# x^T of the last feed-forward by small loads and VectorE transposes in place of TensorE's

## The reference, cut to what matters

```
def _L1_ffn_ref(x, W0, bias0, W1, bias1):
    B, L, H = x.shape
    X = x.reshape(-1, H).astype(jnp.float16)
    D = jnp.dot(X.astype(jnp.float32), W0.T) + bias0       # 512 -> 2048
    D = jax.nn.gelu(D, approximate=False).astype(jnp.float16)
    E = jnp.dot(D.astype(jnp.float32), W1.T) + bias1       # 2048 -> 512
    return E.astype(jnp.float16).reshape(B, L, H)
...
x = _layernorm(x + _L1_ffn_ref(x, ...), axis=-1)
```

## Time and profile before

| | |
|---|---|
| median of 3 runs | 2569.36 us |
| the profiled execution | 2567.99 us |
| its span, first to last instruction | 2566.3 us |
| granted TensorE clock, mean | 0.970 |
| busy: TensorE, VectorE, ScalarE, GpSimd | 2397.7, 1217.7, 808.5, 902.2 us |

### The profile page before, as it was taken

The page is one execution under the profiler, slowest core; times in us unless marked ns, Lnnn a source line. Parts: engine busy times, 40 slices in busy tenths (PEclk is TensorE's granted clock), DMA queues, the critical chain, the costliest instruction groups (busy, mean ns, idle before and its releaser), DMA issues. The chain is left out here.

```text
span 2566.3 us, 39680 instructions
## 1 busy us (share of the span) xinstructions
PE 2397.7 (93%) x12835; PEld 1794.6 (70%) x12835; DVE 1217.7 (47%) x2518; ACT 808.5 (32%) x1371; POOL 902.2 (35%) x1104
## 2 busy tenths in 40 slices
PE   7999899999999958599999995999999979999997
PEld 6887655555555536488888884788888858888886
DVE  3334477777777678511111115676864461111221
ACT  3222255555555521144444442010111012222221
POOL 2000155555555635233333333524334122222221
PEclk9999899999999979799999997999999989999999
DMA  6895254554554235311010103131411151000000
GB/s 238 286 293 180 103 129 118 125 127 119 124 128 119 63 140 196 135 34 49 33 49 33 66 17 128 57 118 46 153 39 69 58 177 33 33 33 33 33 33 33
DMA packets 154745, 255.38 MB, mean 100 GB/s; under 512 B 9904, under 2 KB 47792, under 8 KB 154672
## 3 DMA queue, kind: packets, MB, share of 16 engines
q1 hardware_dynamic: 137712, 208.20, 26.5%
q0 software_dynamic: 6400, 25.26, 3.2%
q10 hardware_dynamic: 10560, 20.97, 2.5%
HBM read 161.59 MB, written 92.27 MB: 99 GB/s over the span
## 5 line engine op out<-in xcount | busy, mean ns | idle before, releaser
L177 DVE CUSTOM_DVE_ANT_0 junk<-psum,causal 128x896 bf16<-128x896 f32 (+7 forms) x512 | 373.7, 751 | 169.9 <-PE psum L828 145.7
L929 ACT ACTIVATE p_probs<-psum 128x512 f32<-128x512 f32 (+1 forms) x640 | 318.0, 555 | 274.9 <-PE psum L841 270.0
L1378 POOL TENSOR_TENSOR p_h_lo<-p_h,p_h_hi 128x512 fp32r<-128x512 f32 x128 | 164.5, 1285 | 325.9 <-ACT p_h_hi L1407 325.9
L841 PE MATMUL psum<-qst,kst 98*128 98x512 f32 (+3 forms) x768 | 223.8, 371 | 6.2 <-POOL p_ones L701 5.7
L2031 POOL CAST p_h<-p_h 128x512 fp32r<-128x512 f16 x128 | 91.4, 714 | 374.2 <-ACT p_h L2055 374.1
L747 POOL TENSOR_SCALAR_AFFINE_SELECT p_probs<-p_probs 128x128 f32<-128x128 f32 x512 | 139.8, 296 | 230.2 <-ACT p_probs L929 227.8
L841 PEld LDWEIGHTS psum<-qst,kst 98*128 98x128 f32 x768 | 132.3, 191 | 111.7 <-DVE rowmax L177 42.7
L828 PE MATMUL psum<-kst,qst 96*128 96x128 f32 (+3 forms) x720 | 208.2, 364 | 0.0
L1075 PE MATMUL psum<-p_xT,p_w_hi 128*128 128x512 f32 x512 | 204.0, 398 | 0.7 <-ACT p_xT L2042 0.7
L1075 PE MATMUL psum<-p_xT_hi,tern 128*128 128x512 f32 x512 | 203.1, 397 | 1.4 <-DVE p_xT_lo L1477 1.4
L1446 PE MATMUL psum<-tern,p_h_hi 128*128 128x512 f32 x512 | 199.5, 390 | 2.3 <-POOL p_h_lo L1378 2.3
(11 more groups left out here) (192 smaller groups left out, 4659.6 us busy)
## 6 DMA issues: line engine op xcount, KB each, us to landing
qst<-q_parts SPq DMA_DIRECT2D x96, 256.0 KB, 4.8
kst<-k_parts SPq DMA_DIRECT2D x96, 256.0 KB, 7.0
q_parts<-p_qk_out SPq DMA_DIRECT2D x32, 512.0 KB, 3.4
k_parts<-p_qk_out SPq DMA_DIRECT2D x32, 512.0 KB, 3.4
ffn_x<-x SPq DMA_DIRECT2D x12, 1024.0 KB, 5.6
p_x<-in_x_t POOLq DMA_DIRECT2D x8, 1024.0 KB, 8.1
v_rows<-p_v_out SPq DMA_DIRECT2D x32, 256.0 KB, 4.0
v<-v_rows SPq DMA_DIRECT2D x16, 512.0 KB, 4.2
```

What stands on the lines that cost most here:

```text
L177: return dve.tensor_tensor_reduce(view(junk[:, 0:n]), bank, view(self.causal[:, SEQ - n:SEQ]), 1.0, FLOOR, ALU.add, ALU.max, self.rowmax[: ...
L841: mm = pe.matmul(psum[:, bank, col:col + CH - q0], kst[s][0:KD + 2, g, j * P:(j + 1) * P], qst[s][0:KD + 2, c, g, q0:CH], start=True, stop ...
L929: act.activation(probs[:, n % 2, g, col:CH], psum[:, banks_of(s, "s", st)[0], col:CH], ACT.Exp, scale=SM_SCALE).then_inc(p_ready, 1)
L1378: pool.tensor_tensor(h_lo[:, m % 2, :], h[:, m % 2, :], f32(h_hi[:, m % 2, :]), ALU.subtract).then_inc(hl_done, 1)
```

## The change

For all chunks but the first, TensorE's transposes, their banks and the cast from `x3` are gone. In their place:

- `load_pieces` issues 16 DMAs per chunk, one per group of 32 features (q) and feature block (k). Each writes 32 partitions with 16 runs of 32 features (128 bytes), so that partition 32q + j holds, for each of the 16 token groups m, the features of token 32m + j. 
- `turn` on VectorE transposes 32x32 squares within these pieces, four instructions of 128x512 fp32, which gives x^T, and casts it to fp16 into `x16` (now feature-major). 
- ScalarE copies `x16` from SBUF to `xT` after the steps t = 10 to 13 instead of from PSUM after t = 9 to 12.

Chunk 1's pieces are issued by ScalarE at the phase's start, behind its copies for chunk 0 and ahead of the Gelu table's load, into `res`; they are turned into `x3[1]` when VectorE has split all weights. The later chunks' pieces are issued by SyncE, those of chunk n + 2 in chunk n, once chunk n + 1 has been cast, ahead of the reload and the store of chunk n. They go to the first two slots of `stage` and are turned into the other two, behind the LayerNorm of chunk n. SyncE's load of `x3[1]` now waits for chunk 1's cast. The first chunk is as before.

```diff
-        T = Banks(nc, ctx, "p6_tbank", psum, 6, 2, 2 * KT)
+        T = Banks(nc, ctx, "p6_tbank", psum, 6, 2, KT)
...
+        BL = 32
+        flat = lambda ap: ap.rearrange("p t d -> p (t d)")
+        second = (flat(res[:, :, :]), x3[1][:, :])
+        later = (flat(stage[:, 0:2, :]), flat(stage[:, 2:4, :]))
+
+        def load_pieces(eng, chunk, dst):
+            for q in range(P // BL):
+                for k in range(KT):
+                    to = dst[q * BL:(q + 1) * BL, k * CH:(k + 1) * CH].rearrange("j (m i) -> j m i", i=BL)
+                    cols = slice(k * P + q * BL, k * P + (q + 1) * BL)
+                    eng.dma_start(to, x3_dram[chunk].rearrange("(m j) d -> j m d", j=BL)[:, :, cols]).then_inc(x_split, 16)
...
@@ sync
+                sp.wait_ge(x_cast, 2)
                 load_x(0, 1)
                 def body(b, last):
                     for c in range(2):
+                        if not last:
+                            sp.wait_ge(x_cast, 2 * b + c + 2)
+                            load_pieces(sp, 2 * b + c + 2, later[0])
                         sp.wait_ge(ln.summed, ln.FROM + CT + 8 * b + 4 * c + 4)
@@ scalar
                 def x_T(b, c, k):
-                    m = KT * c + k
-                    T.wait_full(act, b, m)
-                    T.free(act.activation(xT[:, c, k, :], T.bank(m).bitcast(F16)[:, 0:CH], ACT.Copy), m)
+                    if k == 0:
+                        act.wait_ge(x_cast, 2 * b + c + 1)
+                    act.activation(xT[:, c, k, :], flat(x16[:, :, :])[:, k * CH:(k + 1) * CH], ACT.Copy).then_inc(x_ready, 1)
...
+                load_pieces(act, 1, second[0])
                 act.preload_act_table(ACT.Gelu)
...
-                            if HT // 2 < t <= HT // 2 + KT and not (c and last):
-                                x_T(b + c, 1 - c, t - HT // 2 - 1)
+                            if HT - 2 - KT <= t < HT - 2 and not (c and last):
+                                x_T(b + c, 1 - c, t - HT + 2 + KT)
@@ tensor
-                            if HT // 2 <= t < HT // 2 + KT and not (c and last):
-                                transposes(b + c, 1 - c, t - HT // 2)
@@ vector
+                def turn(chunk, pieces, turned):
+                    dve.wait_ge(x_split, 16 + 16 * KT * (P // BL) * chunk)
+                    for k in range(KT):
+                        part = slice(k * CH, (k + 1) * CH)
+                        dve.transpose(turned[:, part], pieces[:, part]).then_inc(x_turned, 1)
+                    dve.wait_ge(x_turned, KT * chunk)
+                    dve.wait_ge(x_ready, KT * chunk)
+                    dve.tensor_copy(flat(x16[:, :, :]), turned).then_inc(x_cast, 1)
...
+                turn(1, *second)
                 dve.wait_ge(bias_loaded, 16)
...
                         ln.vector_part(dve, 2 * b + c + 1, lambda t: res[:, t, :], lambda t: res[:, t, :])
+                        if not last:
+                            turn(2 * b + c + 2, *later)
```

More of the change, by code:

```diff
@@ L1977, in phase_ffn1 @@
         passed = sem("p6_passed")
-        x_cast = sem("p6_x_cast")
+        x_cast, x_ready = sem("p6_x_cast"), sem("p6_x_ready")
+        x_split, x_turned = sem("p6_x_split", 16), sem("p6_x_turned")
         h_done, h_used = sem("p6_h_done", 2), sem("p6_h_used", 1)
         stored = sem("p6_stored", 1)
+        BL = 32
[8 more added lines that the diff above has]
+                    eng.dma_start(to, x3_dram[chunk].rearrange("(m j) d -> j m d", j=BL)[:, :, cols]).then_inc(x_split, 16)
         with nc.Block() as block:
@@ L2039, in x_T @@
                 def x_T(b, c, k):
-                    m = KT * c + k
-                    T.wait_full(act, b, m)
-                    T.free(act.activation(xT[:, c, k, :], T.bank(m).bitcast(F16)[:, 0:CH], ACT.Copy), m)
+                    if k == 0:
+                        act.wait_ge(x_cast, 2 * b + c + 1)
+                    act.activation(xT[:, c, k, :], flat(x16[:, :, :])[:, k * CH:(k + 1) * CH], ACT.Copy).then_inc(x_ready, 1)
                 for k in range(KT):
-                    x_T(0, 0, k)
+                    T.wait_full(act, 0, k)
+                    act.activation(xT[:, 0, k, :], T.bank(k).bitcast(F16)[:, 0:CH], ACT.Copy).then_inc(x_ready, 1)
+                load_pieces(act, 1, second[0])
                 act.preload_act_table(ACT.Gelu)
@@ L2062, in _, with transposes @@
                 pe.wait_ge(built, 2)
[L2064 to L2067, removed]
+                def transposes(k):
+                    pe.wait_ge(x_cast, 1)
+                    if k >= 2:
+                        pe.wait_ge(x_ready, k - 1)
                     for t in range(CT):
-                        mm = pe.transpose(T.bank(m).bitcast(F16)[:, t * P:(t + 1) * P], x16[:, t, k * P:(k + 1) * P], ident16[:, :])
-                    T.fill(mm, m)
+                        mm = pe.transpose(T.bank(k).bitcast(F16)[:, t * P:(t + 1) * P], x16[:, t, k * P:(k + 1) * P], ident16[:, :])
+                    T.fill(mm, k)
                 def hidden(b, c, t):
                     if t == 0:
-                        for k in range(2):
-                            T.wait_freed(pe, k, 4 * b + 2 * c + 2)
+                        pe.wait_ge(x_ready, KT * (2 * b + c + 1))
                     pe.wait_ge(w_done, blocks.index(("w0", t // 2)) + 1)
@@ L2082, in _ @@
                 for k in range(KT):
-                    transposes(0, 0, k)
+                    transposes(k)
                 hidden(0, 0, 0)
@@ L2119, in _ @@
                 dve.memset(ln.meanvar[:, :, :], 1.0).then_inc(ln.got_mean, CT)
[L2121 to L2127, removed]
+                def turn(chunk, pieces, turned):
[6 more added lines that the diff above has]
+                    dve.tensor_copy(flat(x16[:, :, :]), turned).then_inc(x_cast, 1)
+                dve.wait_ge(x_loaded[0], 16)
+                dve.tensor_copy(flat(x16[:, :, :]), x3[0][:, :]).then_inc(x_cast, 1)
                 for i, (which, n) in enumerate(blocks):
@@ L2138, in body @@
                     for c in range(2):
-                        if not (c and last):
-                            cast(b + c, 1 - c)
                         for a in range(CT):
@@ L2144, in body @@
                             Y.free(dve.tensor_tensor(e16[:, a, :], Y.bank(m), b1r[:, :], ALU.add), m)
+                        dve.wait_ge(x_loaded[c], 16 * b + 16)
                         dve.wait_ge(stored, 1 + 32 * b + 16 * c)
```

## The result

The changed kernel takes 2577.0 us (median of 7 runs, 2574.69 to 2580.27) against 2569.36 (seven runs by now, same median): ratio 1.0032, 95% interval 1.002 to 1.0043. It is slower by 7.6 us, where 2.1 us less was forecast. The profiled execution took 2576.99 us.

The account below looks back on a forecast made before the run. The prediction took TensorE to bound the last feed-forward, apart from its start. Gain -9.1, idle time +4.4 and slow restart +2.6 made -2.1 us: 2567.3 us against the median of 2569.36, range 2561.5 to 2588.

Parts of the forecast that it names:

- The gain: Last feed-forward, TensorE: seven chunks lose four transpose groups each at 0.325 us, 9.1 us in all.
- The price of 16 issues: Phase start, ScalarE's queue: 0.5 us per load issue, 8.0 us in all, ahead of the Gelu table's load.
- The idle time: Phase start: TensorE gets its first h 4.4 us late and idles that long (3.0 and 7.6 at the ends).
- the 2.6 us for the clock: Phase start: TensorE's matmuls restart slowly after the idle time, adding 2.6 us; nothing is the other end.
- the main case: Whole change: 2.1 us less, own range -4 to +3 us, chance 0.42.
- R2: Phase start: the queue fills and ScalarE is held; +15 us with 8 loads held, +3 with 12; chance 0.23.
- The second term of R2: Draining one load: 32 packets per DMA engine, each taking turns with a weight packet, 3.1 us.
- Pieces for chunk 1: Chunk 0: at 30 ns a packet the pieces land at 2113 to 2118, narrowly before the 2120.5 deadline.
- the doubling of the 30 ns: 128-byte packets: read-modify-write might double the price, to about 30 us a chunk; no row showed it.
- R3: Chunk 0, t = 10: chunk 1's pieces come late at 60 ns a packet, +10 us; chance 0.13.
- R4: Steady chunks: above some 130 ns a packet each of six chunks stalls, +20 us or more; chance 0.05.
- Costed at nothing: Beside other work: chunk 1's pieces, steady-chunk loads and the output store, VectorE's turn, ScalarE's copies from SBUF; no cost.

Follow-up runs that it names:

- f1_spread: Against the changed kernel, chunk 1's 16 loads are issued two behind each of chunk 0's Gelus t = 0 to 7; 2559.4 us, 0.9963 of the kernel before.
- d2_wide: Changed kernel with chunk 1's 16 loads of 64 KB in whole 2 KB rows instead of pieces, for timing only; 2566.15 us (one run).
- f2_sync: Changed kernel with chunk 1's 16 loads on SyncE's queue behind the weights, none on ScalarE's; 2559.55 us, 0.9963 of the kernel before.
- d4_alone: Changed kernel, but SyncE issues the weight blocks from the fifth on only when chunk 1's pieces have landed; 2568.74 us (one run).
- d3_four: Changed kernel with chunk 1's same pieces in four loads of 2048 packets instead of 16 of 512, at the same place; 2575.37 us (one run).
- d5_first8: Changed kernel with 8 of chunk 1's 16 loads at ScalarE's place and 8 on SyncE's queue behind the weights; 2565.97 us (one run).

## Why the prediction was wrong, point by point

**The gain: right.** 9.1 us forecast, 9.0 measured in the chunk's length and 9.3 in f1_spread. The chunk went to 58.0 us.

**The price of 16 issues: the step that failed.** "I take 0.5, with 0.41 and 0.7 as ends. Then 16 x 0.5 = 8.0 us." It was 19.48 us. The idle time was 15.2 us where the sum had 4.4, and the 2.6 us for the clock were 2.2. With d2_wide's 0.46 us an issue the sum comes out as forecast, -2.2 against -2.1. The price of an issue was read from rows in which nothing was held, and it is a price for a queue with room. The 2577.0 us lie inside the stated range, but only because the slow rivals had stretched it to 2588; the main case had the wrong sign.

**R2 was the mechanism, with the wrong unit.** It asked how many loads can be outstanding. The nine of the earlier trace rows were the evidence (their issues are 0.37 to 0.67 us, not the "0.4 to 0.5 us only" of the prediction, which decides nothing), but in their whole stretch, 1565 to 1572, the queue moved 1151 packets, 72 per DMA engine; here it was to hold 512. The room lies near 100 to 160 packets per DMA engine: three loads of 32 went in freely, and the first to be held was the fourth (1.04 us here, 1.86 in f2_sync) or the fifth (2.39 in d4_alone). As an estimate, at one load per 1.22 us and 6.3 us to landing about five are under way. The landings of the changed kernel's start:

```profile
p_stage<-in_f_w SPq DMA_DIRECT2D x9, 512.0 KB, 7.3
p_out<-x ACTq DMA_DIRECT2D x16, 64.0 KB, 6.3
```

The second term of R2 was off as well, and the other way: 3.1 us to drain a load was 1.3. The DMA queues in a stretch of the hold (packets, MB, share of 16 engines), weights and pieces:

```profile
q1 hardware_dynamic: 1315, 1.78, 82.7%
q10 hardware_dynamic: 2979, 0.37, 32.9%
```

A piece's packet takes 0.329 x 120 us / 2979 = 13 ns, not 30, and 2979 of them pass beside 1315 of the weights, not one for one. R2's +15 us for eight held loads is therefore two errors that partly cancel. What happened is a room for four or five loads, and 1.2 us on average for each of the sixteen, +8.6 us by the balance. The chance of 0.23 was too small for a queue whose depth no row showed.

The Trainium skill's account (Perfetto Trace Analysis, DMA Instruction — HWDGE (DVE, Sync)), that the issue lasts until the descriptors are generated and that the buffer may be full before, agrees with the trace: issues grew to 2.78 us, and to 6.3 us with four times the packets (d3_four). It was cited, and given too little weight; the same load issued in 0.35 us into a queue with room, so the generating alone isn't what takes long. Its other part, a generator locked for one issuer at a time, does not show in SyncE's issues of the same time:

```profile
L2010 SPq DMA_DIRECT2D p_stage<-in_f_w x10: 367/368/368, 2073.0 to 2094.7; - x10
...
DMA to landing us min/median/max: 5.6/7.1/8.1
```

They stay at 0.37 us while ScalarE is held; those at 2076.37 and 2087.25 fall into issues of ScalarE of 2.05 and 2.78 us. So one queue's full room didn't hold the other.

**Pieces for chunk 1: in time, right, by wrong sizes.** VectorE could start at 2107.07, where the forecast had the landing at 2113 to 2118, and the copy at t = 10 never waited. The price of a piece in the steady chunks, where the pieces are alone (stretch 2176 to 2200):

```profile
q1 hardware_dynamic: 8448, 1.05, 28.1%
...
p_stage<-x SPq DMA_DIRECT2D x16, 64.0 KB, 2.3
```

0.281 x 384 us / 8448 = 13 ns again, 64 KB in 2.3 us. The Trainium skill (DMA: Bandwidth & Descriptors, Specifications) has transfers below 512 B miss the line rate, and the trace agrees: 128 bytes in 13 ns are 10 bytes per ns, against 20 for the weights' 1.37 KB in 68 ns. Whether they are done as read-modify-write, as it says, no run here tells; the doubling of the 30 ns that the prediction feared from it did not come. R3 and R4 rested on a price about three to ten times too high.

**Costed at nothing: right.** Only in chunk 0, behind the 1 MB load of x3[1] in the same queue, were issues of SyncE held (0.80 to 1.88 us), and TensorE waited for nothing there. Stores, reloads, VectorE's turn (3.75 us against 4.4) and ScalarE's copy from SBUF (0.62 against 0.60) show in no wait of TensorE. The weights' blocks land later, 7.3 us after the issue in the row above, and the last is split at 2107.2 instead of 2105.3, without effect.

## What to carry to other kernels

In these runs a DMA issue was cheap only while its queue had room, and the room went by packets: before many small-run loads are put ahead of something urgent, multiply loads by runs, divide by 16 and compare with the 100 or so that went in freely here. What else the DMA engines carry matters as much, because it sets how fast room comes free. An engine that computes should issue such loads between its instructions, where each has its own slack, or leave them to an engine that has nothing behind them. The same loads turned 9.3 us gained into 7.6 us lost by their place alone.

## What the runs showed of the hardware that was not expected

- 128-byte packets took 13 ns each, with the queue alone and with the weights beside it, against 36 ns in a stretch of mostly 512-byte ones.
- The queue of one issuer was held at 1.2 us a load while the other's issues stayed at 0.37 us, on the same DMA engines.
- With the pieces alone on the DMA engines, 16 loads 0.53 us apart were never held (SyncE, steady chunks); beside the weights 9 of 16 issues took over 1 us.
- TensorE's clock fell 0.6 us after work had resumed, behind a gap of 4.33 us (d5_first8); after 3.86 us and 4.84 us (d2_wide) the matmuls were slow from the first.
- VectorE transposed 128x512 fp32 in 32x32 squares in 2.48 us for four, the price of an addition of that size.
